# Order of the gates of tile 1 on VectorE, and a wait of GpSimd on them, in a two-block LoRA kernel

## The reference

```python
def L0(x, language_ids, W, Wr, A, B):             # 8 experts of rank 16
    base = einsum('btd,od->bto', x, W)
    logits = einsum('btd,ed->bte', x, Wr) + one_hot(language_ids, 8)[:, None] * 5.0
    topw, topi = top_k(logits, 2)
    weights = softmax(topw, axis=-1)
    gates = sum(one_hot(topi, 8) * weights[..., None], axis=-2)
    h = einsum('btd,erd->bter', x, A)
    return base + 2.0 * einsum('bter,bte,eor->bto', h, gates, B)

def L1(x, A, B, adapter_ids):                     # 64 adapters of rank 16
    Bx = einsum('bni,bri->bnr', x, B[adapter_ids])
    return einsum('bnr,bor->bno', Bx, A[adapter_ids])

x = x + L0(x, itok_B_0_7, W, Wr, A0, B0)
x = x + L1(x, A1, B1, itok_B_4_50)
```

## Time and profile before

| | us |
|---|---|
| median of 3 timed runs | 97.64 |
| lowest and highest of them | 96.98 and 97.81 |
| profiled execution, its own time | 96.81 |
| its span, first to last instruction | 95.1 |

### The profile page before, as it was taken

One profiled execution on the slowest core, in us unless ns is written; L12 is line 12 of the kernel. 1 busy time (PEld: TensorE's weight loads), 2 busy tenths in 40 slices (PEclk: granted clock), 3 DMA queues, 4 the chain that ended last, 5 costly groups with the idle time before them and its releaser, 6 DMA issues.

```text
span 95.1 us, 2229 instructions
## 1 busy us (share of the span) xinstructions
PE 89.9 (95%) x757; PEld 74.0 (78%) x757; DVE 64.3 (68%) x219; ACT 44.0 (46%) x89; POOL 36.8 (39%) x44
## 2 busy tenths in 40 slices
PE   4999999999999997999999999999999999999960
PEld 1499888787888785888878888887888898898850
DVE  4348989699787029999566279993440569892980
ACT  2663367466999019089395094980293200001200
POOL 5000866669973000499770009992008100000000
PEclk9999999999999999999999999999999999999998
DMA  1998999972037422239448225802321287241066
GB/s 18 357 332 205 296 391 333 359 223 60 0 78 193 152 78 67 47 68 267 190 148 241 59 62 191 295 14 107 73 49 39 65 310 274 90 160 67 0 225 216
DMA packets 15684, 15.21 MB, mean 160 GB/s; under 512 B 10424, under 2 KB 11704, under 8 KB 15288
## 3 DMA queue, kind: packets, MB, share of 16 engines
q1 hardware_dynamic: 14600, 11.63, 39.1%
q0 software_dynamic: 640, 2.10, 7.0%
q10 hardware_dynamic: 432, 1.33, 4.2%
HBM read 10.81 MB, written 4.24 MB: 158 GB/s over the span
## 4 chain that ended last, share of the span: by engine, by line
PE 81%; DMA 8%; DVE 6%; issue 1%; ACT 1%; DVEq 0%
PE main L751 14%; PE main L757 13%; PE main L763 13%; PE side L860 6%; PE main L777 4%; PE main L778 4%; PE main L779 4%; DMA gate_rows<-gate_rows_t 4%; DMA gate_rows_t<-gate_t 4%; PE main L911 3%; PE side L797 3%; DVE xs L622 3%; PE side L888 2%; PE aw_ps L797 2%; PE aw_ps L812 2%; PE aw_ps L829 2%
## 5 line engine op out<-in xcount | busy, mean ns | idle before, releaser
L751 PE MATMUL main<-x_hi,w_hi 128*128 128x512 f32 (+1 forms) x64 | 17.4, 394 | 0.0
L757 PE MATMUL main<-x_hi,w_lo 128*128 128x512 f32 (+1 forms) x64 | 16.8, 385 | 0.0
L763 PE MATMUL main<-x_lo,w_hi 128*128 128x512 f32 (+1 forms) x64 | 16.8, 384 | 0.0
L352 POOL TENSOR_TENSOR x_lo<-xs,x_hi 128x512 fp32r<-128x512 f32 x12 | 15.2, 1288 | 1.2 <-ACT x_hi L391 1.2
L328 POOL TENSOR_TENSOR a_rest<-rows,a_hi 128x512 f32<-128x512 f32 x6 | 7.7, 1294 | 18.3 <-DVE gate_t L558 9.9
L757 PEld LDWEIGHTS main<-x_hi,w_lo 128*128 128x128 f32 x64 | 11.8, 188 | 2.6
L763 PEld LDWEIGHTS main<-x_lo,w_hi 128*128 128x128 f32 x64 | 11.8, 188 | 2.4
L751 PEld LDWEIGHTS main<-x_hi,w_hi 128*128 128x128 f32 x64 | 11.5, 188 | 2.7 <-issue 0.4
L579 DVE TENSOR_TENSOR xs<-main,xs 128x512 f32<-128x512 f32 x15 | 10.0, 685 | 2.5 <-PE main L779 2.4
L450 ACT ACTIVATE down_ops<-down 64x128 fp32r<-64x128 f32 x24 | 7.4, 309 | 6.6 <-DVE down L594 6.2
L391 ACT ACTIVATE x_hi<-xs 128x512 fp32r<-128x512 f32 x16 | 9.0, 622 | 2.5 <-DMA xs<-x_t 2.5
(11 more groups left out here) (129 smaller groups left out, 150.3 us busy)
## 6 DMA issues: line engine op xcount, KB each, us to landing
out_t<-xs SPq DMA_DIRECT2D x16, 256.0 KB, 2.4
xs<-x_t SPq DMA_DIRECT2D x2, 1024.0 KB, 6.1
b1s<-b_t SPq DMA_DIRECT2D x64, 32.0 KB, 1.8
xs<-x_t SPq DMA_DIRECT2D x4, 256.0 KB, 4.2
ws<-w_t SPq DMA_DIRECT2D x4, 256.0 KB, 4.7
xs<-x_t ACTq DMA_DIRECT2D x1, 1024.0 KB, 6.4
gate_rows<-gate_rows_t SPq DMA_DIRECT2D x3, 256.0 KB
b0s<-b_t SPq DMA_DIRECT2D x1, 256.0 KB, 4.9
```

What stands on the lines that cost most here:

```text
L352: nc.gpsimd.tensor_tensor(x_lo[:, t % 2, c], xs[:, t, c], x_hi[:, t % 2, c].bitcast(F32), ALU.subtract).then_inc(x_lo_ready, 1)
L751: nc.tensor.matmul(out_ap, w_hi[:, c, k], x_hi[:, s, k, n], start=(k == 0), stop=False)
L757: nc.tensor.matmul(out_ap, w_lo[:, c, k], x_hi[:, s, k, n], start=False, stop=False)
L763: last = nc.tensor.matmul(out_ap, w_hi[:, c, k], x_lo[:, s, k, n], start=False, stop=False)
```

## The change

On DVE, `gates(1)` moves from behind `add_x1(0, 0)` to `add_x1(0, 3)` and the two `mask_down` of tile 0 to a place ahead of them, right behind `pick` of tile 1. On POOL, a wait for `gate_t_ready` stands behind `x_rest(1, 0)`, and `split_a1(0)` comes ahead of `x_rest(1, 1)`. No instruction is added or removed but the wait.

```diff
@@ -355,8 +355,9 @@
 
             pool.wait_ge(aw_lo_ready, 1)
             x_rest(1, 0)
+            pool.wait_ge(gate_t_ready, 1)
+            split_a1(0)
             x_rest(1, 1)
-            split_a1(0)
             split_a1(1)
             x_rest(1, 2)
             x_rest(1, 3)
@@ -691,6 +692,7 @@
             top_two(logit_b)
             gt_rest(0)
             pick(logit_b)
+            gates(1)
             for t in range(NB):
                 more = t + 1 < NB
                 for c in range(K):
@@ -703,8 +705,6 @@
                 if more:
                     for g in range(t * GPB, (t + 1) * GPB):
                         mask_down(g)
-                    if t == 0:
-                        gates(1)
                     if t + 2 < NB:
                         block_logits(t + 2)
                         top_two(logit_b)
```

## The result

| | before | changed |
|---|---|---|
| median of the timed runs, us | 97.55 (4 runs) | 96.31 (4 runs) |
| lowest and highest, us | 96.98 and 97.81 | 95.90 and 96.64 |
| profiled execution, us | 96.81 | 96.64 |

The account below looks back on a forecast made before the run. PE, busy 95% of the span, was taken as the bound, with one closable gap at the lora of tile 1. 0.90 us won less 0.05 stall gives 0.85: 97.64 to 96.8 us, range 96.0 to 97.5.

Parts of the forecast that it names:

- The bound: PE, busy 95% of the span, has one gap, at the first product of lora(1, 0): 0.90 us to win.
- The move on VectorE: With GpSimd held, gap and picked of tile 1 take 0.17 and 0.23 us; gate_t is ready at 22.17, 5.0 us earlier.
- The cover of 1.40 us: Time given back by gap and picked of tile 1 (0.61 + 0.79 us), hiding the gates' 1.38 us before add_x1.
- Rival D: gap and picked stay long for a reason other than GpSimd; down_part waits 1.3 us, time 98.05; chance 0.05.
- The transfers: SP takes the gates at about 22.7; with 3.57 and 3.59 us gate_rows lands at 29.9, gt_lo 1.6 us early.
- The wait on GpSimd: Five subtractions held until 22.27 end at 28.6; PE wants x_lo(1, 3) at 28.64, no margin left.
- The forecast 0.05 us of stall: PE waiting for x_lo(1, 3) in the third part of base(1, 0); bounds 0 to 0.6 us.
- `gap` of tile 2 sets GpSimd back by 0.17 us: By the skill's exclusion rule, gap of tile 2 delays x_lo(1, 3) by 0.17 us; sum 0.7 instead of 0.85.
- rival E: Later gather becomes the bound through a1_half(3) on ACT ahead of gt_half(1): 1.25 us lost, 98.9; chance 0.06.
- The sum: 0.90 us won at the lora of tile 1, 0.05 lost at x_lo(1, 3): 0.85 us; median 97.64 to 96.8.
- rival A: The forecast itself: the gap at the lora closes, 0.5 to 0.97 us won, about 96.8; chance 0.44.
- rival B: Timed runs' gap is longer through the gates' transfers, by up to 0.83 us; 0.98 to 1.7 us won; chance 0.36.

Follow-up runs that it names:

- the two half changes: On the kernel before: gates(1) moved ahead but GpSimd not held, ratio 1.0366; GpSimd held but the gates not moved, ratio 1.0622.
- the half change: Kernel before with gates(1) moved ahead of the additions but GpSimd not held; ratio 1.0366, 3.6 us slower.

## Why the prediction was right

**The bound.** One gap of PE was there to be closed, and its size was right: 0.90 us in the profiled execution, closed to 0.46 or 0.47 us between the two products in every profile of the changed kernel and in that with the gathers moved. One reading was off, and nothing hangs on it: PE's last product starts at 91.52 us, not near 89.2.

**The move on VectorE.** `gap` and `picked` fell to the forecast 0.17 and 0.23, the gates took 22.85 - 21.46 = 1.39 us for the 1.38 worked out. The cover of 1.40 us sufficed: in the changed kernel's profile the bank was complete at 22.34 + 0.39 = 22.73 and the addition started at 22.77, so nothing of it was left over. Rival D, that the stretching has another reason, fell with the two half changes: GpSimd busy, the stretch is there; GpSimd held, it is gone. The Trainium skill, "SBUF — State Buffer" ("Who interferes with whom"), says that besides operations with two SBUF inputs `tensor_scalar`, too, can contend for the pair of ports that VectorE shares with GpSimd, when its operands meet the conditions of a 2-port mode. `denom` at 1.17 us in the half change agrees, and I had left it out.

**The transfers.** SP was free 1.0 us later than before (the 16 loads took 11.15 us, not 10.15), the write was 1.7 us shorter than forecast. Both terms were wrong and both lay under cover: h is what VectorE waited for, and `gt_lo` was ready at 34.22 + 0.69 = 34.91, 1.7 us before PE started the lora at 36.59; 1.6 had been worked out.

**The wait on GpSimd.** The five subtractions took 29.23 - 22.93 = 6.30 us, for 6.3 forecast. The last weight load of the third part stood at about 28.71 + 3 x 0.23 = 29.40, so 0.17 us were left, and the experiment with one more subtraction measured 0.2. The forecast 0.05 us of stall was not there. That `gap` of tile 2 sets GpSimd back by 0.17 us did not happen either; it came when the last subtraction was already running, so this run doesn't show what it would have done between two of them. The half change shows that VectorE's instructions can slip in between with no delay of GpSimd that could be measured.

**The gathers and ACT** (rival E). ACT stood still for 0.19 us ahead of `a1_half(3)`; the trace names no releaser there, and in the run with one more subtraction it names the gathered rows at the same place (0.18 us). `gt_hi` started at 33.59, when its product (32.85 + 0.70) had just ended. Nothing was lost; by the 1.7 us above, the landing would have had to be some 1.6 us later.

**The sum.** 0.90 - 0.10 = 0.80 us, for 0.85. The term that was mis-sized is the step to the median. I took the profiled execution's gap for all; the timed gain is 1.1 to 1.2 us, above the 0.97 at which rival A ends and inside rival B. The range held because it took in B, to which I had given the smaller chance. The times alone do not decide between the two: both intervals (0.7 to 1.6 and 0.7 to 1.7 us) reach into A, and against the 97.24 us of the kernel before, timed once more, the changed kernel's medians of 96.31 and 96.54 are 0.9 and 0.7 us better, which is A's size.

The profiles show that B's mechanism is real. The second profile of before has 0.38 us more of gap, and its stretch from `down_part` to `down_part` is 46.34 - 23.77 = 22.57 us against 46.01 - 24.73 = 21.28 of the changed kernel's second: 1.29 won, with the wait of 0.29 us inside `down_part` in both, where the first two profiles, with that wait in neither, show 0.80. So the longer gap was worth some 0.4 us in one execution, about half of the 0.83 that I had left open. How many executions have it was not measured. Executions also differ ahead of the stretch, where `down_part` of tile 0 starts anywhere from 23.77 to 24.76 us in these four profiles; behind it all four take 49.2 to 49.3 us. What makes the start differ stays open.

## What to carry to other kernels

When an engine is busy all the time but for one gap, the gap's length is the most that closing it can win; measure it against the same place of the next tile, and in more than one execution if transfers stand in it, because here 0.40 us more of transfer made 0.38 us more of gap. Where short instructions last unusually long, compare their ends with those of a neighbour engine's long ones. Here moving work ahead paid only with the neighbour held for that time, and the held neighbour's own deadline lay 0.2 us away. Before moving a late transfer's start, look at what runs beside it; here taking gathers out of its way won as much, within the scatter.

## What was not expected

The 16 KB write of the gates of tile 1 took 3.6 to 3.8 us from issue to the next step in the three profiles with gathers issued beside it. In the seven without, it took 1.9 us in six (1.87 in the changed kernel, 1.89 with the gathers moved) and 2.2 in one. Gathers are not the only thing that goes with a long write: the write of tile 2, issued right behind the 1 MB load of tile 3, took 46.98 - 42.46 = 4.52 us in the kernel before, with no gather issued for 13 us. A 0.17 us instruction of VectorE was stretched to 1.17 us by a GpSimd instruction of 1.29 us, and GpSimd's pairs of subtractions took 2.51 to 2.55 us with and without such an instruction in between. A wait of PE cost more than its length: after 2.56 us of idle time the granted clock was 0.50 for the next 3 us, and 64 small products took 2.46 us instead of 1.34.
